# Tile-wise opening of a LayerNorm-attention kernel, and a PV bank scaled in the order (query, tile)

## The reference

```
xn  = layernorm(x)
q   = rope(xn @ w_q)               32 heads of 128
k,v = rope(xn @ w_k), xn @ w_v      8 heads, each used by 4 query heads
lk  = rope((xn @ w_lq) @ w_lk)     32 heads, through a latent of 128
lv  = xn @ w_lv                    32 heads
x1  = x + attn(q, k, v) @ w_o + attn(q, lk, lv) @ w_lo      causal softmax
y   = x1 + layernorm(x1) @ W.T + b + routed low-rank term
```

## Time and profile before

| | |
|---|---|
| median of three runs | 2145.01 us |
| the profiled execution | 2144.28 us |
| its span, first to last instruction | 2142.5 us |
| PE busy | 2081.5 us (97%) |
| DVE busy | 1575.7 us (74%) |
| ACT busy | 1141.1 us (53%) |
| POOL busy | 882.2 us (41%) |
| granted TensorE clock, mean | 0.997 |

### The profile page before, as it was taken

How to read it: one execution, slowest core, us unless ns; L and a number is a source line. 1 busy time by engine, 2 the same in 40 slices (tenths; PEclk the granted TensorE clock), 3 DMA queues, 4 the chain that set the end, 5 groups by cost and what they waited for, 6 DMA issues and landing times.

```text
span 2142.5 us, 32460 instructions
## 1 busy us (share of the span) xinstructions
PE 2081.5 (97%) x11236; PEld 1756.5 (82%) x11236; DVE 1575.7 (74%) x2946; ACT 1141.1 (53%) x2502; POOL 882.2 (41%) x693
## 2 busy tenths in 40 slices
PE   5999999999999999999999999999999999999989
PEld 4888888888788888888788888888878888888877
DVE  6777777777777777777777777777777777777775
ACT  3555645555455555555455554555545555555541
POOL 4434444434533444443533444443453344344311
PEclk9999999999999999999999999999999999999999
DMA  2111211111011111111111121111111111111121
GB/s 96 36 37 35 46 25 39 41 36 47 26 42 30 38 46 30 42 34 39 37 36 37 35 47 26 37 42 37 46 27 40 34 34 46 30 41 34 39 51 40
DMA packets 101840, 83.71 MB, mean 39 GB/s; under 512 B 28200, under 2 KB 73896, under 8 KB 101680
## 3 DMA queue, kind: packets, MB, share of 16 engines
q1 hardware_dynamic: 101680, 81.65, 15.3%
HBM read 79.26 MB, written 2.36 MB: 38 GB/s over the span
## 4 chain that ended last, share of the span: by engine, by line
PE 72%; DVE 15%; POOL 6%; issue 4%; ACT 2%; DMA 0%; DVEq 0%; SPq 0%; ACTq 0%
PE scores L414 9%; PE scores L416 9%; PE scores L415 9%; PE bankT L476 8%; PE bankX L414 7%; PE bankX L416 7%; PE bankX L415 7%; PE bankO L414 5%; PE bankO L416 5%; PE bankO L415 5%; DVE rot_half L977 4%; DVE rot_half L976 3%; DVE probs L960 3%; POOL rot L1193 2%; POOL rot L1195 2%
## 5 line engine op out<-in xcount | busy, mean ns | idle before, releaser
L701 ACT ACTIVATE PT_hi<-bankT 128x512 fp32r<-128x512 f32 (+2 forms) x640 | 337.0, 533 | 386.9 <-PE bankO L416 322.8
L966 DVE TENSOR_TENSOR PT_lo<-bankT,PT_hi 128x512 fp32r<-128x512 f32 (+2 forms) x640 | 387.3, 608 | 184.9 <-ACT PT_hi L701 179.9
L760 ACT ACTIVATE probs<-probs,nmax 128x128 f32<-128x128 f32 (+7 forms) x512 | 395.0, 773 | 137.7 <-DVE nmax L960 137.6
L960 DVE CUSTOM_DVE_ANT_0 probs<-scores,mask 128x128 f32<-128x128 f32 (+7 forms) x512 | 381.5, 750 | 66.8 <-PE scores L416 65.7
L476 PE MATMUL bankT<-ident,probs 128*128 128x128 f32 x2304 | 379.0, 273 | 8.0 <-DVE PT_lo L966 2.5
L476 PEld LDWEIGHTS bankT<-ident,probs 128*128 128x128 f32 x2304 | 285.4, 140 | 75.8 <-DVE PT_lo L966 21.0
L1193 POOL TENSOR_TENSOR rot<-rot,cos 128x512 f32<-128x512 f32 x144 | 186.2, 1293 | 217.5 <-DVE rot_half L977 217.5
L1187 POOL TENSOR_TENSOR OT_lo<-o_raw,OT_hi 128x512 fp32r<-128x512 f32 x64 | 82.8, 1294 | 409.8 <-ACT OT_hi L701 409.8
L1195 POOL TENSOR_TENSOR rot<-rot,rot_half 128x512 f32<-128x512 f32 x144 | 205.6, 1428 | 11.3
L701 ACT ACTIVATE OT_hi<-o_raw 128x512 fp32r<-128x512 f32 x128 | 81.0, 633 | 193.8 <-DVE o_raw L1031 148.7
L976 DVE TENSOR_TENSOR rot_half<-rot,sin 64x512 f32<-64x512 f32 x144 | 108.2, 751 | 85.6 <-ACT rot L701 82.2
(11 more groups left out here) (241 smaller groups left out, 5205.6 us busy)
## 6 DMA issues: line engine op xcount, KB each, us to landing
inv_b<-inverses SPq DMA_DIRECT2D x128, 256.0 KB, 3.9
stage<-in_L_attn_w_q SPq DMA_DIRECT2D x32, 256.0 KB, 4.8
stage<-in_L_attn_w_lv SPq DMA_DIRECT2D x32, 256.0 KB, 2.8
stage<-in_L_attn_w_o SPq DMA_DIRECT2D x32, 256.0 KB, 4.9
stage<-in_L_attn_w_lo SPq DMA_DIRECT2D x32, 256.0 KB, 2.6
acc<-in_L_attn_hidden_states SPq DMA_DIRECT2D x2, 1024.0 KB, 7.1
stage<-in_L_attn_w_k SPq DMA_DIRECT2D x8, 256.0 KB, 5.1
stage<-in_L_attn_w_v SPq DMA_DIRECT2D x8, 256.0 KB, 5.5
```

Of the source, the lines that this page charges most:

```text
L701: return act.activation(place, src, ACT.Copy)
L760: act.activation(prob_tile(c, t), prob_tile(c, t), ACT.Exp, bias=nmax[:, c, t:t + 1], scale=-1.0, accum_out=rsum[:, c, t:t + 1]).then_inc( ...
L960: dve.tensor_tensor_reduce(place, src, tile_view(mask[:, S - width:S], c), -SCALE, -MASKED, ALU.add, ALU.min, nmax[:, c, t:t + 1]).then_in ...
L966: dve.tensor_tensor(pt_place(1, hh, w, j), bankT[j % 2][:, block_columns(c, j):CH], f32(pt_place(0, hh, w, j)), ALU.subtract).then_inc(pt_ ...
```

## The change

Opening:
- x comes in eight transfers, each with its own semaphore. The identity matrix comes first of all.
- DVE takes the statistics of each tile as it lands, and those of tiles 4 and 5 before the inverse for tiles 0 to 3.
- All four tiles of a half are normalised in a row, into `probs`, which is not yet in use. The transposes go to four banks (`bankT` twice, `bankO`, `bankX`). All four transposes of the second half come after the projection Wq.
- ACT loads the table for the root at its first instruction, clears OT itself (four copies of a column times 0), and loads the table for the exponential after the second root. POOL clears the rest before it does anything with weights.

Windows: `scale_out` now walks over `bankO` with the tile innermost (a step of 128 words), over `inv_b` in the order in which it lies, and writes `o_raw` in the order (query, tile). The copy to `OT_hi` and both ways of making `OT_lo` read `o_raw` with a step of four words.

```diff
-        x_loaded, w_loaded = [sem("x_loaded0"), sem("x_loaded1")], [sem("w_loaded0"), sem("w_loaded1")]
+        x_loaded, w_loaded = [sem(f"x_loaded{i}") for i in range(NT)], [sem("w_loaded0"), sem("w_loaded1")]
...
                                                   sem("cleared"))
+        tables_loaded = sem("tables_loaded")
...
         f32 = lambda ap: ap.bitcast(F32)
+        x_banks = [bankT[0], bankT[1], bankO, bankX]
+        def x_normalised(made, i):
+            if made:
+                return o_raw[:, i % 2, :]
+            return probs[1][:, i * CH:(i + 1) * CH] if i < 6 else probs[0][:, (i - 6) * CH:(i - 5) * CH]
+        def x_bank(made, i):
+            return bankT[i % 2] if made else x_banks[i % TPC]
...
+        def by_tile(ap):
+            return ap.rearrange("p (t q) -> p t q", q=P)
+        def scaled(w):
+            return o_raw[:, w % 2, :].rearrange("p (q t) -> p t q", q=P)
...
                 tiles = slice(half * TPC, (half + 1) * TPC)
-                sp.dma_start(acc[:, tiles, :], x_in[0, half * CH:(half + 1) * CH, :].rearrange("(i p) d -> p i d", p=P))\
-                    .then_inc(x_loaded[half], 16)
+                for i in range(tiles.start, tiles.stop):
+                    sp.dma_start(acc[:, i, :], x_in[0, i * P:(i + 1) * P, :]).then_inc(x_loaded[i], 16)
...
+            sp.dma_start(ident[:, :], ident_in).then_inc(ident_loaded, 16)
             load_x(0)
-            sp.dma_start(ident[:, :], ident_in).then_inc(ident_loaded, 16)
...
                 pe.wait_ge(xn_made, made + i + 1)
-                if i >= 2:
-                    pe.wait_ge(xt_lo, made + i - 1)
+                ahead = 2 if made else TPC
+                if i >= ahead:
+                    pe.wait_ge(xt_lo, made + i - ahead + 1)
                 for k in range(ND):
-                    mm = pe.transpose(bankT[i % 2][:, k * P:(k + 1) * P],
-                                      o_raw[:, i % 2, k * P:(k + 1) * P], ident[:, :])
+                    mm = pe.transpose(x_bank(made, i)[:, k * P:(k + 1) * P],
+                                      x_normalised(made, i)[:, k * P:(k + 1) * P], ident[:, :])
...
                     project(weights, n, place=four[x]).then_inc(x_ready, 1)
-                    if n == 0 and x < 2:
-                        normalised_transpose(0, TPC + 2 * x)
-                        normalised_transpose(0, TPC + 2 * x + 1)
+                    if n == 0 and x == 0:
+                        for i in range(TPC, NT):
+                            normalised_transpose(0, i)
...
                     act.wait_ge(xt_ready, made + i + 1)
-                    copy(xnT[0][:, :, i * P:(i + 1) * P], bankT[i % 2][:, :].rearrange("p (k n) -> p k n", k=ND))\
+                    copy(xnT[0][:, :, i * P:(i + 1) * P], x_bank(made, i)[:, :].rearrange("p (k n) -> p k n", k=ND))\
...
                     act.wait_ge(o_scaled, unit_no(g, hh, w) + 1 + C_OS)
-                    copy(OT[0][:, kind, c * CH:(c + 1) * CH], o_raw[:, w % 2, :]).then_inc(o_hi, 1)
+                    copy(by_tile(OT[0][:, kind, c * CH:(c + 1) * CH]), scaled(w)).then_inc(o_hi, 1)
+            act.wait_ge(ident_loaded, 16)
+            act.activation(rinv[:, 0, 0:1], ident[:, 0:1], ACT.Sqrt)
+            for half in OT:
+                for kind in range(2):
+                    act.activation(half[:, kind, :], ident[:, 0:1].broadcast_to([P, S]), ACT.Copy, scale=0.0)
...
             root(1, 1)
+            act.activation(rinv[:, 0, 1:2], ident[:, 0:1], ACT.Exp).then_inc(tables_loaded, 1)
...
-            normalised_hi(0, range(TPC, TPC + 2))
...
             first_take(0)
-            normalised_hi(0, range(TPC + 2, NT))
+            normalised_hi(0, range(TPC, NT))
...
         def _(dve):
+            def tile_statistics(tiles):
+                for i in tiles:
+                    dve.wait_ge(x_loaded[i], 16)
+                    dve.bn_stats(stats[:, i, :], acc[:, i, :]).then_inc(dve_chain, 1)
+                chain[0] += len(tiles)
             def statistics(step, half):
+                tile_statistics(range(half * TPC, (half + 1) * TPC))
+                whole_statistics(half)
+            def whole_statistics(half):
                 tiles = range(half * TPC, (half + 1) * TPC)
-                for i in tiles:
-                    dve.bn_stats(stats[:, i, :], acc[:, i, :]).then_inc(dve_chain, 1)
-                chain[0] += TPC
...
             def normalise(made, i):
-                if i >= 2:
+                if i >= 2 and made:
                     dve.wait_ge(xt_ready, made + i - 1)
-                    if made:
-                        dve.wait_ge(xt_used, i - 1)
-                dve.tensor_scalar(o_raw[:, i % 2, :], acc[:, i, :], mv[:, i, 0:1], std[:, 2, i:i + 1],
+                    dve.wait_ge(xt_used, i - 1)
+                dve.tensor_scalar(x_normalised(made, i), acc[:, i, :], mv[:, i, 0:1], std[:, 2, i:i + 1],
...
                 rows = slice(i * P, (i + 1) * P)
-                dve.tensor_tensor(xnT[1][:, :, rows], bankT[i % 2][:, :].rearrange("p (k n) -> p k n", k=ND),
+                dve.tensor_tensor(xnT[1][:, :, rows], x_bank(made, i)[:, :].rearrange("p (k n) -> p k n", k=ND),
...
                 dve.wait_ge(inverses_loaded, 16 * (unit + 1))
-                dve.tensor_tensor(o_raw[:, w % 2, :].rearrange("p (t q) -> p t q", q=P),
-                                  bankO[:, :].rearrange("p (t q) -> p t q", q=P),
-                                  inv_b[:, w % 2, :].rearrange("p (q t) -> p t q", q=P), ALU.mult).then_inc(o_scaled, 1)
+                dve.tensor_tensor(o_raw[:, w % 2, :].rearrange("p (q t) -> p q t", q=P),
+                                  bankO[:, :].rearrange("p (t q) -> p q t", q=P),
+                                  inv_b[:, w % 2, :].rearrange("p (q t) -> p q t", q=P), ALU.mult).then_inc(o_scaled, 1)
...
                 t = slice(c * CH, (c + 1) * CH)
-                dve.tensor_tensor(OT[1][:, kind, t], o_raw[:, w % 2, :], f32(OT[0][:, kind, t]), ALU.subtract)\
+                dve.tensor_tensor(by_tile(OT[1][:, kind, t]), scaled(w), by_tile(f32(OT[0][:, kind, t])), ALU.subtract)\
...
             dve.sem_inc(o_lo[0], C_OL)
-            dve.wait_ge(x_loaded[0], 16)
             statistics(0, 0)
+            tile_statistics(range(TPC, TPC + 2))
             inverse_std(0, 0)
-            normalise(0, 0)
-            normalise(0, 1)
+            for i in range(TPC):
+                normalise(0, i)
+            tile_statistics(range(TPC + 2, NT))
...
                 normalised_lo(0, i)
-                if i < 2:
-                    normalise(0, i + 2)
-            dve.wait_ge(x_loaded[1], 16)
-            statistics(1, 1)
+            whole_statistics(1)
             inverse_std(1, 1)
-            normalise(0, 4)
-            normalise(0, 5)
+            for i in range(TPC, NT):
+                normalise(0, i)
+            dve.wait_ge(tables_loaded, 1)
...
-            normalised_lo(0, 4)
-            normalised_lo(0, 5)
+            for i in range(TPC, NT):
+                normalised_lo(0, i)
             rotate(0, 0, 0, 0)
-            normalise(0, 6)
-            normalise(0, 7)
-            normalised_lo(0, 6)
-            normalised_lo(0, 7)
...
                 at = (ALL, kind, chunk(c))
-                subtract(OT[1][at], o_raw[:, w % 2, :], OT[0][at]).then_inc(o_lo[1], 1)
+                subtract(by_tile(OT[1][at]), scaled(w), by_tile(OT[0][at])).then_inc(o_lo[1], 1)
...
             pool.sem_inc(o_lo[1], C_OL)
-            weights_low(0, 0, Wq)
-            weights_low(1, 1, Wk)
-            for tensor in (*PTD, *OT, *Wo, *Wlo):
+            for tensor in (*PTD, *Wo, *Wlo):
...
             ins.then_inc(cleared, 1)
+            weights_low(0, 0, Wq)
+            weights_low(1, 1, Wk)
```

## The result

The changed kernel takes 2121.47 us (median of four runs, 2120.74 to 2122.93); the kernel before, beside it on the same chip, takes 2145.63 us (four runs, 2144.95 to 2147.25). The ratio is 0.989, with a 95% interval of 0.9879 to 0.9902. The forecast was 2126 us, in a range of 2111 to 2150.

What follows compares the result with a forecast made beforehand. PE, busy 2081.5 of 2142.5 us, was taken as the bound. From 2144.28 us, -9.6 (opening), -21.3 (shorter scaling) and +12 (window 3) gave 2125.4, or 2126 us as median; range 2111 to 2150.

Steps and rivals of the forecast that it cites:

- The opening, first half: Start to projection Wq: DVE's stall behind POOL's clears goes, so Wq starts at 18.0 us instead of 24.16, 6.2 us.
- The step that was waved off: Opening loads: finer transfers of x and the root's table loaded ahead give nothing, since the inverse waits for tile 5.
- The opening, second half: Wq to Wlq: Wlq starts near 27.8 us instead of 37.33, 9.5 us; whole opening -9.6 us, bounds -6 and -12.
- `scale_out`: Scaling of bankO on DVE in each window: falls from 1067 to 692 ns, the step in PSUM being free.
- First PV matmul and maxima: PE's waits in the windows: shorter scaling saves 12.0 us at first PV matmuls and 9.3 us at scores behind window 1.
- `OT_hi` on ACT, and the wait into window 3: ACT's copy from o_raw takes 375 ns more, delaying DVE's low part into window 3: 32 x 0.375 = +12 us.
- `OT_lo` into window 1: DVE's low part there takes 375 ns more, but PE waits for POOL's LKT_lo instead: no cost.
- `OT_lo` on POOL: POOL's low part, 64 times: between 0 and 1.3 us more each, hidden because its readers come a head later: nothing.
- the first rival: ACT reads SBUF with a step at no cost, so the 12 us do not come: 2114 us; chance 0.27.
- the second: Rival: the step costs DVE as much in PSUM as in SBUF, and ACT pays too: 2159 us, slower; chance 0.15.
- third: Rival: the step costs DVE as much in PSUM, but ACT pays nothing: 2147 us, no discernible change; chance 0.15.
- the fourth: Rival: the opening gives nothing, as tile 5 or ACT's clears are late and Wq's gap reappears: 2136 us; chance 0.08.

Runs made afterwards that it cites:

- the contiguous 685 ns: Changed kernel with the inverses stored in DRAM by tile, so bankO, inv_b and o_raw are accessed without a step: 2347.81 us, ratio 1.0943.

## Why the prediction was right, step by step

- **The opening, first half.** Right. The inverse was put at 10.7 us and started at 10.63, the first normalisation at 11.8 and came at 11.76, the first projection at 18.0 and came at 17.60. That the stall of 5.25 us belongs to POOL's clears is shown by putting them back: 5.7 us.
- **The step that was waved off.** "Finer transfers [...] give nothing here" was wrong by the 1.7 us that two transfers cost (2.1 us in the profile). The tables, in the same sentence, do give nothing.
- **The opening, second half.** Wlq was put at 27.8 us and came at 26.73, so the term of -9.6 us (37.33 - 27.8 is 9.5) measured -10.6, and -11.0 at the first `scale_out`. Of the first us, 0.4 is the first projection; the rest is the clock, which rose while that projection ran (its matmuls go from 0.43 to 0.23 us apart at 21.5 us, where before that was at 27.8). The prediction had it in its bounds and not in its sum.
- **`scale_out`.** 692 ns forecast, 681 measured. The lower end was the right one to take, and the contiguous 685 ns show that nothing is left in it.
- **First PV matmul and maxima.** Right. -12.0 and -9.3 forecast. Summed from the starts of the matmuls, the waits for the bank went from 14.3 to 1.9 us and those for a maximum from 8.9 to none: -12.4 and -8.9.
- **`OT_hi` on ACT, and the wait into window 3.** The term of the sum that was mis-sized. Forecast +375 ns, from DVE's SBUF read; measured +515 (633 to 1148). The +375 ns for `OT_lo` on DVE were about right as the price of the step (0.69 to 1.09 us). But in this place it grew by 0.26 only, since it took 0.84 before, 0.15 more than its shortest; no run isolates what those 0.15 us were. Both together lengthen the row by 0.42 us a head, and the distance of the matmuls by 0.38, against 0.375 forecast: that this came out so close is luck, as the two errors cancel. The +12 us were 32 times 0.375. The wait grew in 31 heads and by 14.2 us, more than forecast, but in 7 of them the wait for `QT_lo` behind it gave 5.2 us back, which the forecast had not seen: 9.0 us net. The mechanism is right, as the old order in window 2 alone shows.
- **`OT_lo` into window 1** costs nothing, as forecast: window 1 is 0.4 us longer over all heads.
- **`OT_lo` on POOL.** Forecast between 0 and 1.3 us more, hidden; measured 0.27 more, hidden.
- **The rivals.** `OT_hi` at 1148 ns excludes the first, `scale_out` at 681 the second and third, the first projection the fourth. In time alone the result lies between the forecast (2126) and the first rival (2114); the durations decide.

The sum for the profiled execution was 2125.4 us, and the span of 2119.5 with the 1.8 us around it is 2121.3: 4.1 us lower. Counted to the first `scale_out`, 1.4 of that is the opening (11.0 instead of 9.6). 2.5 are the windows (11.8 instead of 9.3), the net of the +12 that came as 9.0 and of 0.5 more in front of the output tile. 0.2 lies behind the last `scale_out`.

## What to carry to other kernels

In each of these kernels a step between two layouts was paid somewhere: list the instructions that could pay it, and give it to the one whose lateness nobody waits for, place by place, since one of four places here wanted the other choice. Before taking a wait away, look for the chain that ends just behind it and starts ahead of it: only the difference of the two is to be won. Read from the code who consumes an instruction's result before moving it, since 0.2 us to spare and a whole head look the same in a list of waits. And look at the granted clock beside the waits: a kernel that makes PE wait can lose more than the wait.
